# Mixtures of sixteen experts in 128-row tiles ordered by tables, resident second-layer weights, third mixture's tiles following the second's

## What is computed

```python
slot = flat_e * capacity + pos
packed = buf[:E * capacity].reshape(E, capacity, d)
h = gelu(einsum('ecd,edf->ecf', packed, w1) + b1)          # 128 -> 512
expert_out = einsum('ecf,efd->ecd', h, w2) + b2            # 512 -> 128
x = x + 0.5 * (gates * expert_out of the two experts, summed)
```

## Time and profile before

| | |
|---|---|
| runs | 1433.98, 1438.44, 1439.25 us, median 1438.44 |
| profiled execution, its own time | 1434.23 us |
| its span, first to last instruction | 1432.4 us, mean granted TensorE clock 0.930 |
| PE busy | 1176.8 us (82%) |
| DVE busy | 861.8 us (60%) |
| ACT busy | 748.4 us (52%) |
| POOL busy | 696.6 us (49%) |
| DMA | 220.10 MB, mean 154 GB/s |

### The profile page before, as it was taken

The page is one execution under the profiler, slowest core; times in us unless marked ns, Lnnn a source line. Parts: engine busy times, 40 slices in busy tenths (PEclk is TensorE's granted clock), DMA queues, the critical chain, the costliest instruction groups (busy, mean ns, idle before and its releaser), DMA issues.

```text
span 1432.4 us, 27517 instructions
## 1 busy us (share of the span) xinstructions
PE 1176.8 (82%) x7620; PEld 793.1 (55%) x7620; DVE 861.8 (60%) x2897; ACT 748.4 (52%) x1707; POOL 696.6 (49%) x933
## 2 busy tenths in 40 slices
PE   4399797899999999999689878419999777479994
PEld 3299786222223232222379778417889655357894
DVE  7533666888899999988333565722225696522135
ACT  4255453477767767767445545314445566334441
POOL 3776343213233454524754466563455277635553
PEclk9999998799999999999989999759999988589997
DMA  9687667535435435352357666424568131145586
GB/s 297 169 217 217 181 189 225 161 92 165 138 97 157 136 77 144 98 151 75 89 161 192 174 180 182 135 79 140 169 190 269 48 126 36 48 132 166 176 268 201
DMA packets 176707, 220.10 MB, mean 154 GB/s; under 512 B 25040, under 2 KB 126032, under 8 KB 176560
## 3 DMA queue, kind: packets, MB, share of 16 engines
q1 hardware_dynamic: 144880, 174.80, 43.6%
q0 software_dynamic: 17856, 36.74, 7.5%
q10 hardware_dynamic: 13824, 6.82, 1.6%
HBM read 148.25 MB, written 69.76 MB: 152 GB/s over the span
## 4 chain that ended last, share of the span: by engine, by line
PE 53%; DVE 20%; POOL 8%; issue 6%; DMA 5%; ACT 5%; SPq 2%; DVEq 1%; ACTq 0%; POOLq 0%
PE PS L1483 16%; PE PS L1493 16%; DVE arena L2422 6%; POOL dispatched L807 6%; PE PS L1671 5%; PE PS L1647 5%; PE PS L1461 3%; ACT arena L1195 2%; DVE X L1958 2%; PE PS L1655 2%; PE PS L1633 2%; DVE BST L1948 1%; DMA qk_products<-arena 1%; DVEq L2216 1%; DMA arena<-dispatched 1%
## 5 line engine op out<-in xcount | busy, mean ns | idle before, releaser
L1070 ACT ACTIVATE arena<-PS,arena 128x128 f32<-128x128 f32 (+2 forms) x824 | 295.6, 419 | 368.7 <-PE PS L1483 353.2
L829 POOL DMA_INDIRECT expert_out<-arena x302 | 291.6, 965 | 319.1 <-issue 151.3
L1195 ACT ACTIVATE arena<-PS 128x512 f32<-128x512 f32 x512 | 283.9, 597 | 134.4 <-PE PS L1647 133.5
L1493 PE MATMUL PS<-arena 128*128 128x128 f32 (+1 forms) x2416 | 309.4, 277 | 14.7 <-DVE arena L2227 14.2
L1483 PE MATMUL PS<-arena 128*128 128x128 f32 (+2 forms) x1648 | 314.4, 335 | 4.9 <-ACT arena L1070 3.5
L2422 DVE TENSOR_REDUCE arena<-PS 128x2 f32<-128x1024 f32 x256 | 301.1, 1218 | 26.2 <-PE PS L1657 25.0
L1493 PEld LDWEIGHTS PS<-arena 128*128 128x128 f32 x2416 | 294.7, 193 | 29.0 <-issue 18.8
L2227 DVE TENSOR_TENSOR arena<-PS,arena 128x128 f32<-128x128 f32 (+2 forms) x206 | 73.0, 354 | 312.0 <-PE PS L1493 310.6
L1483 PEld LDWEIGHTS PS<-arena 128*128 128x128 f32 x1648 | 237.8, 197 | 39.3 <-issue 9.1
L807 POOL DMA_INDIRECT dispatched<-arena x192 | 186.0, 969 | 81.7 <-issue 55.7
L1647 PE MATMUL PS<-arena 96*128 96x512 bf16 x512 | 173.0, 389 | 12.7 <-ACT arena L1195 6.7
(11 more groups left out here) (273 smaller groups left out, 1171.7 us busy)
## 6 DMA issues: line engine op xcount, KB each, us to landing
arena<-experts SPq DMA_DIRECT2D x64, 578.0 KB
arena<-experts SPq DMA_DIRECT2D x142, 256.0 KB
qk_products<-arena SPq DMA_DIRECT2D x48, 384.0 KB
arena<-qk_products SPq DMA_DIRECT2D x64, 288.0 KB
YC<-expert_out SPq DMA_DIRECT2D x48, 256.0 KB
dispatched<-FILL SPq DMA_DIRECT2D x32, 322.5 KB, 2.5
arena<-dispatched SPq DMA_DIRECT2D x142, 64.5 KB
arena<-qk_products SPq DMA_DIRECT2D x64, 128.0 KB, 5.1
```

The costliest lines, as they stand in the source:

```text
L829: pool.indirect_dma_start(YK, bass.IndirectOffsetOnAxis(ap=ID[:, s:s + 1], axis=0), YS[:, s, :], None).then_inc(s_yo[r], 16)
L1070: act.activation(bent(f, tau)[:, q, 0:N], bank(q, 0, N), func, bias=bias).then_inc(s_g, 1)
L1195: act.activation(PT[:, G % 2, j, k, :], bank(4 + k % 2), ACT.Exp, scale=float(1.0 / np.sqrt(HD))).then_inc(s_exp, 1)
L1493: mm = pe.matmul(bank(6, P * s, P * s + P), bent(f, tau)[:, q, P * s:P * s + P], downs(f, tau, q), start=(q == 0), stop=(q == FC - 1))
```

## The change

- **Tiles.** The mixtures of 16 have 79 tiles of 128 rows, in the order of tables as the mixtures of 8 have; a first table on five batches orders their first 25 tiles, the main table the other 54. `late_table` is gone. The tables take a broadcast over the 16 experts, a clamp of the expert's blocks at five and a clamp of the row.
- **Weights.** Only up-weights (256 KB) are loaded for each tile, into the same ring of six. Second-layer weights and biases of all 16 experts (322 KB each) are resident; SP loads one at every third tile of the second mixture from tile 12. Rings of rows (8), turned rows and hidden rows (4) and up-weights (6) count through all mixtures.
- **Third behind second.** Step 77 (71 tiles and `REST` = 6) is the third's tile 0, so its tiles 0 to 16 run inside the second mixture's loop, which ends at step 93, while batches 5, 6 and 7 are still routed (starts 68, 74, 79). SP waits for the first table and the 40 sends of five batches before the third's tile 0, and for the main table and all sends before tile 25. POOL sends the first five batches in the second mixture, one behind each scatter from tile 37, and the later three in the third, ahead of scatters 1, 7 and 12.
- **Last mixture.** The same first table is made in the linear layer at i = 5, so tiles start on five batches; main table, Exp and gates come in its steps 2 to 8. Six batches are combined during tiles instead of four.
- **Steps of a routed batch.** They are split over more steps: the gather's halves at c and c + 1, moments at c + 1, scores at c + 8, choice at c + 9.
- **Others.** `fill_stack` fills quarters, sixteen of them from step 27. Loads of YC in the mixtures of 16 go from ACT's queue to SP's. `moments` and `inverse_deviation` of batch 3 move from the linear layer's first step into the third mixture.

The diff, cut to its core:

```diff
-MAIN, SHORT = 3, S1 - 3
-MOE = [..., dict(E=E1, S=MAIN, tiles=2 * E1)]
+MOE = [..., dict(E=E1, S=S0, tiles=TOKENS * 2 // (S0 * P) + E1 - 1)]
-FRONTS = 4
+FRONTS, LAST_FRONTS = 4, 6
+KNOWN1, SOON1 = 5, 25
+REST = 6
...
+            def rows_in(f, tau, buf, experts, last):
+                g, soon = on_all(f, tau), early_of(f)
+                t, n = (TS0, tau) if tau < soon else (TS, tau - soon)
+                row = sp.value_load(t[n:n + 1, 0:1], min_val=0, max_val=last)
+                if g >= XRING:
+                    sp.wait_ge(s_yc, g - (XRING - 1))
+                sp.dma_start(XP[:, g % XRING, :], buf[bass.ds(row, P), :]).then_inc(s_rows[g % XRING], 16)
+                if g >= UPS:
+                    sp.wait_ge(s_h, (g - (UPS - 1)) * FC)
+                sp.dma_start(ups(f, tau), experts[...]).then_inc(s_we[g % UPS], 16)
...
             def sixteen(L):
-                for tau in range(RING):
-                    expert_in(tau)
-                sp.wait_ge(s_disp, sent_for(L))
...
+                sp.wait_ge(s_soon, f + 1)
+                sp.wait_ge(s_first, soon_sent(L))
+                for tau in range(tiles):
+                    if tau == soon:
+                        sp.wait_ge(s_tiles, f + 1)
+                        sp.wait_ge(s_disp, sent_for(L))
+                    rows_in(f, tau, buf, ex1_in, SPARE1_AT)
+                    for b in range(fronts_of(L)):
+                        if front_of(b) + 2 == tau:
+                            wait_outputs(sp, f, wide_to(b))
+                            load_outputs(sp, L, b)
...
+        NEXT = MOE[0]["tiles"] + REST
+        def tile_at(L, c):
+            f = ffn_of(L)
+            if c < moe_of(f)["tiles"]:
+                return f, c
+            if carries(L) and c >= NEXT:
+                return f + 1, c - NEXT
...
         def last_step(L):
-            return place_of(L, NG - 1)
+            return place_of(L, NG - 1) + 4
...
+                early = 2 * GT * KNOWN1
+                sent = early if handed(L) else 0
                 for tau in range(tiles):
+                    if handed(L):
+                        while sent < 2 * NT and place_of(L - 1, sent // (2 * GT)) <= NEXT + tau:
+                            send_next(L, sent)
+                            sent += 1
                     scatter(tau)
-                    if carries(L) and tau < tiles - 8 and place_of(L, sent // (2 * GT)) <= tau:
-                        send_next(sent)
+                    if carries(L) and sent < early and place_of(L, sent // (2 * GT)) < tau:
+                        send_next(L + 1, sent)
                         sent += 1
...
+                        for b in starting(L, c):
+                            gather(f, b, 0)
+                        for b in starting(L, c - 1):
+                            gather(f, b, 1)
                         for b in starting(L, c - 8):
                             scores_in(b, E1, bank(5, 0, GT * E1), n + b)
+                        for b in starting(L, c - 9):
+                            chosen_out(b, E1, n + b)
+                            more = add_chosen(b, E1, n + b)
...
+                        if c == place_of(L, KNOWN1 - 1) + 1:
+                            first_sums(f + 1, bank(5, 0, KNOWN1 * E1))
...
                     if batch(i + 1):
                         features(i + 1)
-                    if i == 0:
-                        moments(FRONTS - 1)
-                        inverse_deviation(FRONTS - 1)
...
+                    if i == KNOWN1:
+                        first_table(f, bank(4, 256, 256 + KNOWN1 * E))
```

More of the change, by code:

```diff
@@ L746, in sixteen @@
+                for b in range(fronts_of(L), NG):
+                    wait_outputs(sp, f, wide_to(b))
                     load_outputs(sp, L, b)
@@ L1121, in first_middle @@
                     act.activation(QP[:, 1, w, :], QR[:, w, :], ACT.Copy).then_inc(s_mid0, 1)
-                for c in range(begin(L), last_step(L) + 1 if carries(L) else tiles):
-                    if c < tiles:
-                        gelus(c)
+                for c in range(begin(L) + handed(L), last_step(L) + 1 if carries(L) else tiles):
+                    gelus(c)
                     if prepares(L):
@@ L1455, in tile_turn @@
+                pe.wait_ge(s_sum, f + 1)
+                pe.matmul(out.rearrange("p (a b) -> p a b", b=E), ones_bf[:, :],
+                          SUM[:, 1:NG + 1, 0:E], start=True, stop=True).then_inc(s_counts, 1)
             def tile_turn(f, tau):
-                T0, r, S = TILES0[f], tau % XRING, size(f, tau)
-                pe.wait_ge(s_rows[r], 16 * row_loads(f, tau))
-                if tau > 0:
-                    pe.wait_ge(s_xpc, T0 + tau)
-                for s in range(S):
-                    mm = pe.transpose(bank(4, P * s, P * s + P), XP[:, r, s, 0:D], ident)
@@ L1576, in open_keys_values @@
                     mm.then_inc(s_lk, 1)
-                def find(tau):
-                    if E == E0 and tau < tiles:
-                        find_expert(f, tau, early_tiles(L))
-                if L == 0:
-                    pe.wait_ge(s_soon, first_kind(f) + 1)
-                find(begin(L))
-                lead = lead_of(f)
-                for tau in range(begin(L), begin(L) + lead + 1):
-                    turn(tau)
-                hidden(begin(L))
-                find(begin(L) + 1)
+                if not handed(L):
+                    find(begin(L))
+                    for c in range(begin(L), begin(L) + DEEP - 1):
+                        turn(c)
+                    hidden(begin(L))
+                    find(begin(L) + 1)
                 for c in range(begin(L) + 1, last_step(L) + 1 if carries(L) else tiles + 1):
-                    if c + lead < tiles:
-                        turn(c + lead)
+                    turn(c + DEEP - 2)
                     if carries(L):
@@ L1595, in moe @@
                             carried_logits(b)
-                    if c < tiles:
-                        hidden(c)
+                    hidden(c)
                     if carries(L):
```

717 lines of the change are left out of this document (366 added, 351 removed).

## The result

The changed kernel takes 1451.86 us (median of 4 runs, 1450.09 to 1456.01) against 1438.85 for the kernel before: ratio 1.0098, 95% interval 1.0077 to 1.0120. It is slower by 1%, where no change was forecast. Measured once more with the later experiments it gave 1450.96, ratio 1.0099 (1.0071 to 1.0127). Its profiled execution has a span of 1450.5 us, 18.1 over that of before; the difference of the medians is 13, since the profiled execution of before (1434.23) lies at the low end of its runs.

The account below looks back on a forecast made before the run. PE was taken to bound the mixtures' tiles, with uncovered routing and sends in the holes before the third and last mixtures. Terms summed to −3.8 us on 1434.23, 1434 on the median's scale; forecast 1433, range 1411 to 1453.

Parts of the forecast that it names:

- signs of being wrong: Third mixture under 180 us, over 205 or at clock 0.5; last mixture's first hidden matmul over 8 us behind last placing.
- Fills, −3.6: First mixture: quarter fills last 0.88 us and hide under a tile, where PE waited 0.91 behind half fills: −3.6 us.
- Second mixture, −5: Split routing steps save 1.65 us a batch, −8 in all; the third's first table adds +3: −5 us.
- the first table, "+3": Second mixture: the third's first table goes into steps 68 to 71, beside the last started batch: +3 us.
- The hole, 20.5 to the first hidden: Between second mixture's last tile and third's first hidden matmul: 20.5 us afterwards, with 8 sends left, against 57 before.
- The third's tiles, +1 for hole and tiles: Third mixture's tiles sum to 191.3 us; its last matmul 211.8 after the second's end, against 211.2 before: +1.
- Routing over the cover and the collision: Third's tiles: routing and main table beyond what tiles hide, 12.6 us; batch 6's start colliding with the last table, 2.5.
- Linear layer, +2.5: Batch 3's moments and inverse deviation leave its first step, −2.5 us; the added first table costs +5.
- Start of the last mixture, −14.2; its tiles, +21: Last mixture: 3.2 us from last placing to first hidden matmul instead of 17.4; tiles take 172 us against 151.0.
- Tail, −5.5: End of kernel: with two batches left instead of four for two buffers, both YC loads start at once: −5.5 us.
- The rival on the other side: Third's first tiles stay at the lower 1.2 GHz clock, +1.9 us each; ten such tiles give 1453; chance 0.18.
- Short matmuls: Rival: by the skill page's gaps, 128-column matmuls cost more per column than the tile pace says; near 1590 us; chance 0.02.

Follow-up runs that it names:

- `unsplit`: The changed kernel with VectorE's steps of a routed batch put back as they were, not split: 1460.41 us, ratio 1.0155; measured again 1457.79, ratio 1.0146.
- `order`: The changed kernel with VectorE adding the bias of the second mixture's last tile before computing the third's first table, not behind it: 1448.34 us, ratio 1.0066.
- `sends`: The changed kernel with GpSimd's eight remaining sends ahead of the scatter of the second mixture's last tile, not behind it: 1446.03 us, ratio 1.0056.
- `rest22`: The changed kernel with the third's tile 0 at step 93 instead of 77, so all routing lies ahead of its tiles: 1445.90 us, ratio 1.0048.
- `last4`: The changed kernel with four batches instead of six combined during the last mixture's tiles, as before: 1450.19 us, ratio 1.0103.

## Why the prediction was wrong
The sum was −3.8; the profiled executions differ by +18.1, the medians by +13. Of the 21.9 us between the sum and the profile, 8.8 lie in the second mixture, 8.6 in the hole and the third's tiles, and 4.2 in the linear layer. None of the signs of being wrong that the prediction named showed: the loss came from parts that it had priced too low, not from a rival. By its terms:

- **Fills, −3.6.** Right: −4.7 in the tiles, −4.4 alone.
- **Second mixture, −5.** Wrong: +3.8, of which +1.5 in tiles 0 to 27, −3.2 in tiles 27 to 69 and +5.6 at the last tile. Two steps failed. The split was priced at 1.65 a batch, 8 in all, and its tiles gave 3; the other 4 to 5 that it is worth (`unsplit`) lie elsewhere, 2 to 3 of them at the third's start. Why the sum of steps was too high for these tiles is not shown. And the first table, "+3" beside the last started batch, cost 5.6 between tiles 69 and 70. The prediction counted it as work over the cover of a tile; at the last tile there is no next tile to cover it, and the table and an inverse deviation stand whole on the way to the scatter and the eight sends. `order` and `sends` show it. The cause of the +1.5 was not tried. The loads of second-layer weights begin in these tiles: the three kernels without them take 64.25 to 64.43, the fifteen with them 64.6 to 66.2, which points at the loads; no run takes them out alone.
- **The hole, 20.5 to the first hidden.** Right from tile 70's add: 21.0. From tile 70's matmul it is 28.2, and the difference is the wait at the last tile, told above.
- **The third's tiles, +1 for hole and tiles.** Wrong: 218.7 from the second's last add to the third's, against 209.1, so +9.6. Of that, 2.1 is the prediction's reading of before: it took 211.2, from the last matmul to the end of a window. Its own figure for after was 211.8, 6.9 too low, nearly all in the tiles (197.8 against 191.3). Routing over the cover and the collision, 12.6 and 2.5, were right in sum: 15.1, and 15.3 measured (by `rest22`). The step that failed is the rest. Without routing, in `rest22`, the third takes 182.5, where the prediction's other terms (162 for the tiles, 2 of cold clock, 10 for four combined batches, 2.2 of openings) give 176.2. By its adds, the first output takes 5.5, tiles 3 to 5 are 3.8 over the pace of 2.03, and tiles 49 to 67, where the four batches are combined, 15 over it: the start is 3.6 and the combined batches are 2.8 above their terms. The statement that what is won in the hole is given back was right and too mild: in the changed kernel the overlap alone is a loss of 6, though repaired it is a gain.
- **Linear layer, +2.5.** Low: +3.3 and, in the execution at the lower clock, +6.7. The parts were both off: the moments and the deviation taken out of its first step gave 1.0, not 2.5 (75.3 to 74.3 from the third's last add to the numerators of batch 5), and the table cost 6.4 in its step, near the 7 of the text, of which the next step handed back 2.5; +5 was taken for it.
- **Start of the last mixture, −14.2; its tiles, +21.** Right: −14.4 and +21.1.
- **Tail, −5.5.** Right in size (−4.5), wrong in cause, so the size was luck: with four batches left, as before, 3.4 of the 4.5 stay (`last4`).

The rival on the other side had the time (1453) and the wrong mechanism. The third's start is at the lower clock only for the hole and its first tiles (0.52 from 930.9 to 940.9), and then at 1.00:

```profile
909.00:934.00 25.00, 4.47 (x19) 3.89 (x19) 7.26 (x43) 2.33 (x5) 8.61 (x9) 0.50 0.38 109
930.90:940.90 10.00, 7.86 (x42) 7.53 (x42) 6.51 (x42) 6.27 (x16) 0.49 (x1) 0.52 0.64 167
940.00:990.00 50.00, 44.77 (x364) 41.51 (x362) 32.04 (x170) 29.44 (x91) 37.39 (x39) 1.00 0.62 165
```

By the terms above, the larger part of the slower side came from VectorE's chains instead: tables and deviations ahead of the few short steps for which PE, GpSimd and SyncE wait. Short matmuls did not cost what the Trainium skill, "TensorE: Matmul & The Clock Gate", section "Back-to-back issue gap", would give. The prediction put that at a time near 1590; the time is 1452, and the pace of 2.03 a tile is that of the first mixture before the change, 2.05.

## What to carry to other kernels
Work that hides under a tile in mid-loop stands whole on the path at the loop's last tile: look there first, at what every other engine has queued behind that tile's output. Before overlapping a serial stretch with the next stage, ask what bounds it; here it was one queue of sends, and starting on the early sends removed 25 of 55 us with no overlap, while the overlap put the routing on the same VectorE that fed the tiles. Try a large change's small parts alone: two of them, put into the kernel before, gave a kernel faster than both.

## What was not expected of the hardware
The granted clock in the linear layer differs from one execution to the next with the same code: 0.61 between 1205 and 1228 in the first profile of the changed kernel, 0.82 in the same step of its second profile, and 0.83 in that of `sends`. There the step took 20.6 and 20.4 us instead of 24.55:

```profile
1204.70:1225.30 20.60, 10.68 (x62) 8.67 (x60) 15.19 (x80) 13.20 (x33) 15.53 (x26) 0.82 0.10 33
...
1199.00:1220.00 21.00, 11.46 (x65) 9.30 (x63) 15.74 (x84) 13.13 (x33) 15.97 (x26) 0.83 0.11 36
```

This stretch thus differed by 4 us between profiles, about a third of the whole change. What sets the clock there was not tried.
